# Turning normalised tokens: TensorE's transposes replaced by an SBUF exchange and VectorE's 32 by 32 transposes

## The reference

```
def _L0_attn_ref(x, Wg, bg, Wo, bo):
    g = jax.nn.sigmoid(jnp.einsum('bld,ed->ble', x, Wg) + bg)
    a = 1.0 - g
    b = g * x
    _, h = jax.lax.associative_scan(combine, (a, b), axis=1)
    return jnp.einsum('bld,ed->ble', h, Wo) + bo
...
x = x + _layernorm(_L0_attn_ref(_layernorm(x, axis=-1), ...), axis=-1)
x = x + _layernorm(_L0_ffn_ref(_layernorm(x, axis=-1), ...), axis=-1)
```

## Time and profile before

| | us |
|---|---|
| median of 3 runs | 1164.3 (1164.17 to 1164.88) |
| the profiled execution | 1166.17 |
| its span, from the first to the last instruction | 1163.0 |

### The profile page before, as it was taken

One profiled execution on the slowest core, in us unless ns is written; L12 is line 12 of the kernel. 1 busy time (PEld: TensorE's weight loads), 2 busy tenths in 40 slices (PEclk: granted clock), 3 DMA queues, 4 the chain that ended last, 5 costly groups with the idle time before them and its releaser, 6 DMA issues.

```text
span 1163.0 us, 24424 instructions
## 1 busy us (share of the span) xinstructions
PE 1142.6 (98%) x7549; PEld 1020.4 (88%) x7549; DVE 991.5 (85%) x2741; ACT 742.1 (64%) x1375; POOL 690.1 (59%) x792
## 2 busy tenths in 40 slices
PE   8999999999999999999999999999999999999996
PEld 4788898888988898888888888988898888899996
DVE  6888988888888988989898888888888987688885
ACT  4366666666656666666666666656666666678782
POOL 3556567675656666565657665656666664414444
PEclk9999999999999999999999999999999999999998
DMA  9121110100111111111101101111111100335430
GB/s 262 58 100 56 55 46 35 43 27 30 36 36 36 36 36 36 36 36 36 36 19 35 34 23 33 36 36 36 36 36 36 36 18 20 114 114 191 145 130 34
DMA packets 59428, 65.09 MB, mean 56 GB/s; under 512 B 7835, under 2 KB 55629, under 8 KB 59268
## 3 DMA queue, kind: packets, MB, share of 16 engines
q1 hardware_dynamic: 52228, 59.36, 15.8%
q0 software_dynamic: 7168, 5.34, 1.5%
HBM read 40.19 MB, written 38.76 MB: 68 GB/s over the span
## 4 chain that ended last, share of the span: by engine, by line
PE 90%; DVE 5%; POOL 2%; ACT 1%; issue 1%; DMA 0%; DVEq 0%; POOLq 0%; ACTq 0%
PE psY L1430 12%; PE psY L1433 11%; PE psY L1432 11%; PE psH L1324 11%; PE psH L1325 11%; PE psH L1326 10%; PE psA L1324 5%; PE psA L1325 5%; PE psA L1326 5%; PE psT L1380 3%; PE psT L1337 2%; DVE st L859 1%; PE psT L1393 1%; PE psT L1395 1%; PE psA L1498 1%
## 5 line engine op out<-in xcount | busy, mean ns | idle before, releaser
L621 ACT ACTIVATE hid<-psH,biasT 128x512 f32<-128x512 f32 (+1 forms) x312 | 202.9, 650 | 217.6 <-PE psH L1326 215.2
L1430 PE MATMUL psY<-W_hi,hid_hi 128*128 128x256 f32 x1168 | 336.1, 288 | 0.6 <-DVE hid_lo L1012 0.5
L1433 PE MATMUL psY<-W_hi,hid_lo 128*128 128x256 f32 x1168 | 330.3, 283 | 0.0
L1432 PE MATMUL psY<-W_lo,hid_hi 128*128 128x256 f32 x1168 | 330.2, 283 | 0.0
L399 POOL TENSOR_TENSOR rstd<-veps,mhalf 128x4 f32<-128x4 f32 (+2 forms) x103 | 141.4, 1373 | 163.2 <-DVE nmean L871 163.2
L1012 DVE TENSOR_TENSOR hid_lo<-hid,hid_hi 128x512 fp32r<-128x512 f32 (+1 forms) x308 | 200.6, 663 | 42.5 <-ACT hid_hi L626 35.8
L1324 PE MATMUL psH<-xfT_hi,W_hi 128*128 128x512 f32 (+1 forms) x624 | 235.9, 378 | 0.3 <-ACT hid L621 0.2
L1325 PE MATMUL psH<-xfT_lo,W_hi 128*128 128x512 f32 (+1 forms) x624 | 234.9, 376 | 0.0
L1326 PE MATMUL psH<-xfT_hi,W_lo 128*128 128x512 f32 (+1 forms) x624 | 232.7, 373 | 0.0
L1430 PEld LDWEIGHTS psY<-W_hi,hid_hi 128*128 128x128 f32 x1168 | 222.7, 191 | 9.9 <-DVE hid_lo L1012 1.6
L1432 PEld LDWEIGHTS psY<-W_lo,hid_hi 128*128 128x128 f32 x1168 | 223.0, 191 | 5.9
(11 more groups left out here) (173 smaller groups left out, 2176.8 us busy)
## 6 DMA issues: line engine op xcount, KB each, us to landing
xin<-L_attn_x SPq DMA_DIRECT2D x32, 512.0 KB, 3.4
stage<-L_ffn_w SPq DMA_DIRECT2D x16, 1024.0 KB, 5.2
out<-outt SPq DMA_DIRECT2D x31, 512.0 KB, 2.8
xbuf<-zrow SPq DMA_DIRECT2D x1, 2590.0 KB, 16.5
xin<-xbuf SPq DMA_DIRECT2D x8, 259.0 KB, 4.9
stage<-L_ffn_ow SPq DMA_DIRECT2D x2, 1024.0 KB, 8.5
xbuf<-x,idx POOLq DMA_INDIRECT x128, 2.1
b_b<-L_ffn_b SPq DMA_DIRECT2D x1, 1024.0 KB, 6.5
```

Source lines behind the costliest of these rows:

```text
L621: act.activation(hid[j % 2][:, at:n], psH[:, j % 2, at:n], ACT.Relu, bias=bias).then_inc(s_hid, 1)
L1430: pe.matmul(dst, hi, w[0][:, j, :], start=(j == 0 and (tail or t % 2 == 0)), stop=False, skip_group_check=True)
L1432: pe.matmul(dst, hi, w[1][:, j, :], start=False, stop=False, skip_group_check=True)
L1433: last = pe.matmul(dst, lo_, w[0][:, j, :], start=False, stop=(j == HC - 1), skip_group_check=True)
```

## The change

1. For groups 4 to 31 TensorE's eight transposes are gone. SyncE instead issues 16 transfers within SBUF, one for each pair (a, b) of partition quarters: the square of 32 by 32 at rows b and columns a, in each of the 8 blocks of 128 columns of tok, goes to rows a and columns b of a buffer tok_blocks. Each transfer covers 32 partitions with 8 runs of 128 bytes each. The buffer lies in memory of the first expert's weights (W1_lo), which isn't in use before the experts.
2. VectorE then turns every square in its place, two transposes of 128x512 from tok_blocks into psT (`turn_blocks`), after low(2) and before place. It waits for all 16 transfers.
3. SyncE's step begins with the exchange of `far` (called turn there), ahead of the store of `prev` and the load.
4. veps and nmean of all norms but the very last tiles are made by GpSimd, with two operations at the head of `deviation` and `deviation2`; VectorE's `moments` ends with the aggregations.
5. In GpSimd's step norm0(far) stands ahead of deviation(3, prev).

```diff
@@ SyncE
+            def exchange_blocks(g):
+                i, v = g
+                src = tok[:].rearrange("p t d -> p (t d)").rearrange("p (n c) -> p n c", c=P)
+                dst = tok_blocks.rearrange("p t d -> p (t d)").rearrange("p (n c) -> p n c", c=P)
+                sp.wait_ge(s_tok, cnt(g, 1, 1))
+                for a in range(P // SQ):
+                    for b in range(P // SQ):
+                        sp.dma_start(dst[a * SQ:(a + 1) * SQ, :, b * SQ:(b + 1) * SQ],
+                                     src[b * SQ:(b + 1) * SQ, :, a * SQ:(a + 1) * SQ]).then_inc(s_blocks[v], 16)
...
-            def step(i, u):
-                prev, nxt, far = grp(i, u, -1), grp(i, u, 1), grp(i, u, 3)
+            def step(i, u, later=True):
+                prev, nxt, turn, far = grp(i, u, -1), grp(i, u, 1), grp(i, u, 2), grp(i, u, 3)
+                if later and live(turn, NG):
+                    exchange_blocks(turn)
                 if live(prev, NG):
                     store(prev)
@@ GpSimd
             def deviation(k, g, n, extra=0, t0=0):
+                pool.wait_ge(s_ag[k], cnt(g, 1, 1) + extra)
+                pool.sem_inc(s_held, 1)
+                pool.tensor_scalar(veps[k][:, t0:n].unsqueeze(2), mv[k][:, t0:n, 1:2], EPS, None, ALU.add).then_inc(s_ve[k], 1)
+                pool.tensor_scalar(nmean[k][:, t0:n].unsqueeze(2), mv[k][:, t0:n, 0:1], -1.0, None, ALU.mult)
                 pool.wait_ge(s_ve[k], cnt(g, 1, 1) + extra)
...
+                if live(far, NG):
+                    norm0(far)
                 if live(prev, NG):
                     deviation(3, prev, TG, t0=sure(prev))
-                if live(far, NG):
-                    norm0(far)
@@ VectorE
             def moments(k, g, n, base=0, t0=0):
                 dve.wait_ge(s_st[k], cnt(g, 1, 1) + base)
+                dve.wait_ge(s_nm[k], cnt(g, 1, 0) + base)
...
-                dve.tensor_scalar(veps[k][:, t0:n].unsqueeze(2), mv[k][:, t0:n, 1:2], EPS, None, ALU.add)
-                dve.tensor_scalar(nmean[k][:, t0:n].unsqueeze(2), mv[k][:, t0:n, 0:1], -1.0, None, ALU.mult)\
-                    .then_inc(s_ve[k], 1)
...
+            def turn_blocks(g):
+                i, v = g
+                dve.wait_ge(s_blocks[v], landed((i - 2, v), (P // SQ) ** 2))
+                for c in range(DC):
+                    dve.transpose(psT[:, c, :], tok_blocks[:, :, c * P:(c + 1) * P]).then_inc(s_T0, 1)
...
                 low(2)
+                if ahead:
+                    turn_blocks(far)
                 if run and up:
                     place(now)
@@ TensorE
-                    if j == 3 and ahead:
-                        transposes0(far)
```

More of the change, by code:

```diff
@@ L26 @@
 QUAD = P // TG
+SQ = 32
 EPS = 1e-5
@@ L124, in hid_of @@
             return (hid_hi, hid_lo)[p][j % 4]
+        tok_blocks = late[1][:, 0:TG * D].bitcast(F32).rearrange("p (t d) -> p t d", d=D)
         ysb = sb("ysb", [P, TG, D])
@@ L210, in sandwich_kernel @@
         s_T0 = sem("s_T0")
+        s_blocks = sems("s_blocks")
         s_xn_hi = sem("s_xn_hi")
@@ L323, in _ @@
             load((1, 0))
-            step(0, 0)
+            step(0, 0, later=False)
             sp.wait_ge(s_ow_hi, 4)
@@ L329, in _ @@
             load_w2((0, 0))
-            step(0, 1)
+            step(0, 1, later=False)
             with sp.Fori(1, NG // 2 - 2) as i:
```

6 lines of the change are left out of this document (4 added, 2 removed).

## The result

The changed kernel takes 1399.5 us (median of 4 runs, 1398.9 to 1400.2) against 1164.5 for the kernel before in the same session. The ratio is 1.202, 95% interval 1.200 to 1.204. The forecast was 1286 with a range of 1219 to 1402 and a chance of 0.90 for slower: the sign and the mechanism came true, and the time lies at the upper edge of the range, 113 us over the forecast.

The account below looks back on a forecast made before the run. TensorE's own stream (31.15 us a step) bounds the kernel; the change closes a loop of six links, 35.6 us, adding 4.45 us to 27 steps plus 2.3 for the first, 122 in all: 1286 us, range 1219 to 1402.

Parts of the forecast that it names:

- the mechanism: Loop VectorE, GpSimd, SyncE's 16 transfers, VectorE: one round of 35.6 us sets the step, against 30.23 of TensorE work.
- covered: norm3 on ScalarE, relu(2) and residual2 come later but stay hidden; in a 31 us step norm3 starts about 1 us later.
- hidden now: GpSimd's path to tok: tokens normalised long before TensorE turns them, VectorE never waiting; spare time in no row of waits.

Follow-up runs that it names:

- reordered: Changed kernel with all 16 transfers, GpSimd's step in another order (norm0 a step earlier, scatters a step later, state_lo last): 1183.1 us, ratio 1.015.
- four_wide: Changed kernel with 4 transfers over 128 partitions instead of 16 over 32, same runs and bytes, tokens not turned rightly: 1226.6 us, ratio 1.053.
- statistics_alone: Changed kernel without the exchange (TensorE turns all groups) and with norm0 behind deviation(3) again, leaving only GpSimd's statistics: 1210.2 us, ratio 1.041.
- kept_clock: Changed kernel with 16 matmuls without use on TensorE ahead of layer2(3) of each step, where it stands idle: 1394.7 us, ratio 1.197.

## What to carry to other kernels

Before a transfer is put between two engines, add up the whole round: what waits for it on the receiving queue, what that releases, and whether this leads back to the sender. A latency in such a loop is paid in every step, however little of each engine it uses, and with the same 16 transfers outside the loop 19 of the 235 us were left (reordered). Price an exchange by the number of its transfers at the spacing that rows show, with the upper end open. When a part of a change is "covered", work out the loop that it would lie on if the main effect were gone; here two more closed at 32.4 to 32.6 us, one over norm3 and one over the statistics of stage 3, tok and TensorE. And measure the slack of a path that is "hidden now" in two steps in a row, not in one.

## What the runs showed of the hardware

- SyncE issues transfers within SBUF 0.65 us apart when they stand in line (16 in 10.42 us). 64 runs each instead of 256 make it 0.64 (10.21), and four times the runs in each of four transfers 0.71 (4 in 2.81). A single store or load takes 0.39 to 0.41. Why the exchange's issues are longer than those is open; no run varied the shape alone.
- An exchange of 512 KB in runs of 128 bytes lands 1.9 us behind its last issue; in four transfers instead of 16 it is 2.5 us (four_wide). Issued 16 times in 10.42 us it keeps the DMA engines busy for 0.31 of the time at 50 GB/s, by an estimate 12 to 13 ns a packet. Four transfers keep them fully busy, at 170 GB/s.
- VectorE's 32 by 32 transpose of 128x512 fp32 elements from SBUF to PSUM takes 0.71 us on the mean.
- GpSimd's operations on 128x4 elements vary: the same veps takes from 0.23 to 1.08 us within two steps of statistics_alone, so that eight of them a step cost more than their shortest times say. That VectorE's use of SBUF is the cause is likely from the earlier trace rows, but wasn't tested.
- TensorE's last matmul ended at 503.77, its granted clock fell from 1.00 to 0.50 between 506 and 507, matmuls began again at 509.56, and the clock was back at 513. In a stretch that is covered this costs nearly nothing (kept_clock, 5 us).
